# A two-block perceiver kernel on one Trainium2 core: the keys and values of every fourth sequence of the second cross-attention projected during the first feed-forward layer and kept in DRAM

## What is computed

```
x = x + L0_xattn(layernorm(x), ctx)
x = x + L0_attn(layernorm(x))
x = x + L0_ffn(layernorm(x))
x = x + L1_xattn(layernorm(x), ctx)
x = x + L1_attn(layernorm(x))
x = x + L1_ffn(layernorm(x))
```

```
def act_qdq(x):
    scale = max(max(abs(x)) / 32767, 1e-12)
    return clip(round(x / scale), -32768, 32767) * scale
...
x = act_qdq(x);  up = act_qdq(x @ w_up.T);  gate = act_qdq(x @ w_gate.T)
sig = round(sigmoid(gate) * 65536) / 65536
gate = act_qdq(gate * sig);  o = act_qdq(gate * up)
return o @ w_down.T
...
q = x1 @ Wq.T + bq;  k = x2 @ Wk.T + bk;  v = x2 @ Wv.T + bv
attn = softmax(q k^T / 4) per head;  return (attn v) @ Wo.T + bo
```

## Time and profile before

| what | value |
|---|---|
| median of 3 runs | 1647.59 us (1645.24 to 1649.38) |
| the profiled execution | 1646.64 us |
| its span on the core | 1644.9 us |
| PE, PEld busy | 1472.1 us (89%), 1131.8 us (69%) |
| DVE, ACT, POOL busy | 898.0 us (55%), 718.2 us (44%), 498.4 us (30%) |
| mean granted clock of TensorE | 0.967 |
| the chain that ended last, by engine | PE 71%, DVE 16%, issue 5%, POOL 4%, ACT 3% |

### The profile page before, as it was taken

How to read it: one execution, slowest core, us unless ns; L and a number is a source line. 1 busy time by engine, 2 the same in 40 slices (tenths; PEclk the granted TensorE clock), 3 DMA queues, 4 the chain that set the end, 5 groups by cost and what they waited for, 6 DMA issues and landing times.

```text
span 1644.9 us, 32798 instructions
## 1 busy us (share of the span) xinstructions
PE 1472.1 (89%) x12556; PEld 1131.8 (69%) x12556; DVE 898.0 (55%) x1896; ACT 718.2 (44%) x1761; POOL 498.4 (30%) x693
## 2 busy tenths in 40 slices
PE   3999996982899999999995788789999999999999
PEld 3877774432777777777773566538876885886787
DVE  3898896388445555655554778734224323422432
ACT  3887775486445555555551555422212211221221
POOL 2345551001036855854551878500000000000000
PEclk9999999995999999999996999989999999999999
DMA  7000000001031151135100000013421340342230
GB/s 280 21 10 2 1 0 1 1 0 34 7 129 46 60 221 38 45 141 204 39 25 1 1 1 0 1 45 112 157 103 45 136 178 13 134 150 87 90 135 13
DMA packets 49501, 111.39 MB, mean 68 GB/s; under 512 B 4240, under 2 KB 6800, under 8 KB 46864
## 3 DMA queue, kind: packets, MB, share of 16 engines
q1 hardware_dynamic: 49424, 110.36, 19.1%
HBM read 99.86 MB, written 10.49 MB: 67 GB/s over the span
## 4 chain that ended last, share of the span: by engine, by line
PE 71%; DVE 16%; issue 5%; POOL 4%; ACT 3%; DMA 1%; SPq 0%; DVEq 0%; POOLq 0%; ACTq 0%
PE ps L831 22%; PE ps L479 14%; PE ps L677 7%; PE ps L683 7%; PE ps L485 4%; PE ps L703 4%; PE ps L882 3%; DVE R L1491 3%; PE ps L714 2%; PE ps L655 2%; DVE amax L1373 2%; DVE nmx L1251 1%; DVE R L1442 1%; DVE R L1410 1%; PE ps L579 1%
## 5 line engine op out<-in xcount | busy, mean ns | idle before, releaser
L831 PE MATMUL ps<-R 128*128 128x256 f32 x1792 | 388.6, 379 | 3.5 <-DVE R L1620 3.5
L831 PEld LDWEIGHTS ps<-R 128*128 128x128 f32 x1792 | 340.0, 190 | 52.3 <-issue 6.5
L479 PE MATMUL ps<-R 128*128 128x128 f32 (+1 forms) x1344 | 307.4, 388 | 6.4 <-DVE R L1369 4.8
L479 PEld LDWEIGHTS ps<-R 128*128 128x128 f32 x1344 | 190.4, 194 | 119.6 <-issue 109.4
L1752 POOL TENSOR_TENSOR R<-R,c_inv 128x1024 f32<-128x1024 f32 x64 | 121.1, 1893 | 186.4 <-DVE c_inv L1528 186.4
L1090 ACT ACTIVATE R<-ps,c_nmx 128x257 f32<-128x257 f32 x256 | 118.0, 474 | 99.1 <-DVE c_nmx L1515 99.1
L1491 DVE COPY R<-ps 128x512 f32<-128x512 f32 x128 | 88.3, 690 | 106.8 <-PE ps L703 105.6
L677 PE MATMUL ps<-R,x_wk 128*128 128x256 f32 x512 | 128.8, 394 | 0.0
L683 PE MATMUL ps<-x_wv,R 128*128 128x256 f32 x512 | 121.1, 379 | 0.0
L1828 POOL TENSOR_SCALAR g_ve<-g_mv 128x4 f32<-128x4 f32 x4 | 0.9, 236 | 345.9 <-DVE g_mv L1582 345.9
L677 PEld LDWEIGHTS ps<-R,x_wk 128*128 128x128 f32 x512 | 92.7, 191 | 16.9 <-issue 0.8
(11 more groups left out here) (198 smaller groups left out, 2486.8 us busy)
## 6 DMA issues: line engine op xcount, KB each, us to landing
R<-quadrant_sums SPq DMA_DIRECT2D x32, 1024.0 KB, 6.9
R<-in_f_hq SPq DMA_DIRECT2D x32, 768.0 KB, 4.6
R<-in_ctxT SPq DMA_DIRECT2D x64, 257.0 KB, 2.7
R<-in_f_hq SPq DMA_DIRECT2D x8, 1024.0 KB, 8.2
quadrant_sums<-R SPq DMA_DIRECT2D x8, 1024.0 KB, 8.2
R<-in_f_w SPq DMA_DIRECT2D x3, 1024.0 KB, 7.0
R<-in_ctxk SPq DMA_DIRECT2D x16, 128.0 KB, 2.1
out<-x SPq DMA_DIRECT2D x4, 512.0 KB, 2.6
```

Source lines behind the costliest of these rows:

```text
L479: r = mm(dst, w[:, ki, fo * P:(fo + 1) * P], src[:, ki, :], start=(ki == 0), stop=(ki == KI - 1))
L831: r = mm(ps[:, 4 * (g % 2) + bk, half * HALF:(half + 1) * HALF], f_wr[g % 3][:, w, ki * P:(ki + 1) * P], src[:, k, ki, :], start=(ki == 0) ...
```

## The change

Sequences 3, 7, 11, ... (u = 3 of each tile, 16 in all) are no longer projected in the loop. They are numbered j = 0 to 15 and projected in `L0_ffn`: j = 0 to 9 between the gate and up projections and `c_last`, 10, 11 and 12 after `f0_down(0)`, `(1)` and `(2)`, and 13 to 15 after `f0_down(3)`. For each, SP loads the context (`load_ahead`), GpSimd shifts it (`shift_ahead`), TensorE projects it, ACT copies keys and values into one of three small buffers (`stage_ahead`), and SP stores both in the DRAM tensor `kv_ahead` (`store_ahead`). In the loop SP loads keys and values of tile i back, 256 KB each, into `c_kT[3]` and `c_v[3]`. Step u = 1, which projected u = 3, now projects nothing. At u = 2 the first half of the values stands ahead of the turning. Some semaphores are merged, and `ctx_last` is loaded at the start of the program.

```diff
@@ SP
+            def load_ahead(j):
+                sp.dma_start(a_ctx[j % 3], A["ctxT"][SPT * j + 3, :, :, 0:S - 1]).then_inc(ctxk_in[j % 3], 16)
+            def store_ahead(j):
+                sp.wait_ge(k_copied, ahead_no(j))
+                sp.dma_start(kv_ahead[j, :, 0:2, :], a_kT[j % 3]).then_inc(ahead_stored[j % 3], 16)
+                sp.wait_ge(v_copied, ahead_no(j))
...
+            for j in range(AHEAD):
+                if j + 3 < AHEAD:
+                    sp.wait_ge(v_ready, ahead_no(j))
+                    load_ahead(j + 3)
+                if j == 3:
+                    sp.wait_ge(f0_gj, 2)
...
+                if j >= 1:
+                    store_ahead(j - 1)
@@ PE, c_step
-                more = not (last and u >= 2)
+                more = u != 1 and not (last and u >= 2)
...
+                if more:
+                    pe.wait_ge(v_copied, rest_no(done - 1))
+                    if u == 2:
+                        c_values((u + 2) % SPT, 0)
                 if behind:
                     pe.wait_ge(c_nrm, n)
                     c_turn_probs(n - 1, (u + 1) % 2, 0)
                 if more:
-                    pe.wait_ge(v_copied, n + 2)
-                    for c in range(2):
+                    for c in range(1 if u == 2 else 0, 2):
                         c_values((u + 2) % SPT, c)
@@ PE, around f0_down
+            for j in range(AHEAD_PAUSE):
...
+                    pe.wait_ge(v_copied, ahead_no(j - 4))
+                keys_ahead(j, 2 * (j % 4))
+                values_ahead(j, 2 * (j % 4) + 1)
...
             f0_down(0)
+            ahead(10)
             f0_down(1)
+            ahead(11)
             c_turn(0)
             f0_down(2)
+            ahead(12)
             c_query(0)
             f0_down(3)
+            for j in range(13, AHEAD):
+                ahead(j)
@@ ACT
-            for f in range(3):
+            for f in range(2):
                 f0_up_int(f)
             act.wait_ge(f0_scale, 4)
...
+            for f in range(2, NF0):
+                stage_ahead(f, 2 * (f % 4))
+                f0_up_int(f)
+                f0_gate_int2(f)
+            for j in range(NF0, AHEAD_PAUSE):
+                stage_ahead(j, 2 * (j % 4))
@@ POOL
-            for k in (QX, QG, QU, QS):
-                all_max(k)
+            all_max(QX)
+            pool.wait_ge(c_last_in, 16)
+            for j in range(3):
+                shift_ahead(j)
+            all_max(QG)
+            shift_ahead(3)
+            all_max(QU)
+            shift_ahead(4)
+            all_max(QS)
+            for j in range(5, AHEAD_PAUSE):
+                shift_ahead(j)
...
             for u in range(3):
                 c_shift(u, 0)
+            for j in range(AHEAD_PAUSE, 13):
+                shift_ahead(j)
             all_max(QO)
```

More of the change, by code:

```diff
@@ L202, in perceiver, with ahead_no, first_no, rest_no @@
         c_nmr = sb("c_nmr", [P, 1])
+        AHEAD, AHEAD_PAUSE = T, 10
+        def ahead_no(j):
+            return j + 1 if j < AHEAD_PAUSE else j + 3
+        def first_no(u):
+            return AHEAD_PAUSE + u + 1
+        def rest_no(m):
+            return AHEAD + m + 1
+        def ahead_shift_no(j):
+            return j + 1 if j < AHEAD_PAUSE else j + 4
+        a_ctx = [view(WT + 4608 + 512 * i, KI, S - 1) for i in range(3)]
+        a_kT = [view(WT + at, KI, S - 1) for at in (0, 1024, 1536)]
+        a_v = [view(WT + at, 512) for at in (512, 2560, 2048)]
         HALF, QUAD = BLK // 2, 4 * BLK
@@ L358, in perceiver @@
         N1 = 2 * T
+        NORMS = 4 * T
         WOUT = {X0: x0_wo, A0: a0_wout, A1: a1_wout}
@@ L433, in _ @@
                     n = SPT * i + u
-                    sp.wait_ge(v_ready, n + 1)
-                    sp.dma_start(c_ctx[u], A["ctxT"][n + SPT]).then_inc(ctx_in[u], 16)
+                    if u < 3:
+                        sp.wait_ge(v_ready, rest_no(3 * i + u) if i or u == 2 else first_no(u))
+                        sp.dma_start(c_ctx[u], A["ctxT"][n + SPT]).then_inc(ctx_in[u], 16)
+                    if u == 1 and i:
+                        load_keys(i)
+                    if u == 3 and i:
+                        load_values(i)
                     if n == 3:
@@ L902, in _ @@
         def _(act):
-            for m in free["act"]:
+            for m in ():
                 act.sem_inc(m, 1)
@@ L1095, in c_step @@
                 c_exps(u % 2, n)
-                more = not (last and u >= 2)
+                more = u != 1 and not (last and u >= 2)
                 if more:
-                    c_keys(u % 2, n + 2)
-                if more:
+                    m = rest_no(3 * i + 2 if u == 0 else 3 * i + u + 1)
+                    c_keys((u + 2) % SPT, m)
                     after(act, c_o, n - 1)
-                    c_values((u + 2) % 4, n + 2)
+                    c_values((u + 2) % SPT, m)
                 if u == 1 and not last:
@@ L1534, in _ @@
             f0_add(0)
-            for u in range(2):
+            for u in (0, 1, 3):
                 r = v.tensor_copy(c_kT[u][:, :, S - 1], colb[:, BK1, :])
@@ L1748, in c_step @@
                 n = SPT * i + u
-                if not (last and u >= 1):
-                    c_shift((u + 3) % SPT, i + (u + 3) // SPT)
+                if u >= 1 and not last:
+                    c_shift(u - 1, i + 1)
                 pool.wait_ge(c_rinv, n + 1)
@@ L1771, in _ @@
                 c_shift(u, 0)
+            for j in range(AHEAD_PAUSE, 13):
+                shift_ahead(j)
             all_max(QO)
             c_rsqrt(0)
+            shift_ahead(13)
             c_bias(0)
+            for j in range(14, AHEAD):
+                shift_ahead(j)
             for u in range(SPT):
```

196 lines of the change are left out of this document (134 added, 62 removed).

## The result

| | before | after |
|---|---|---|
| median | 1646.69 us (1645.24 to 1649.38, 4 runs) | 1699.24 us (1698.77 to 1700.09, 4 runs) |
| span of the profiled execution | 1644.9 us | 1697.4 us |
| mean granted clock of TensorE | 0.967 | 0.955 |
| first scores of the loop (n = 0) | 464.27 | 505.00 |
| from there to the scores of n = 62 | 403.1 | 415.4 |

The changed kernel takes 1.0318 times as long (95% interval 1.03 to 1.0336), 52.5 us more. The forecast was 1683 us and the range 1660 to 1694: the direction was right, the time is 16 us above the forecast and 5 above the range.

The account below looks back on a forecast made before the run. Bound by waits for DVE, ACT and GpSimd's maxima before the down projection, by TensorE in it, by DVE's chain in the loop. 1646.64 + 21.2 + 21.9 - 7.2 = 1682.5, median 0.95 higher: 1683 us; range 1660 to 1694.

Parts of the forecast that it names:

- GpSimd's switches: In L0_ffn, changing between maxima and ordinary operations costs 7.04 us each way; QO and f0_down(0) come 21.2 us later.
- The last link: Ahead of QO: load 12, needing the projection of j = 9, lands near 425.5, shift 12 ends near 426.5, QO starts 433.5.
- (a): In L0_ffn, the switch towards the maxima is free, only the one away from them costs: 1663 us, chance 0.17.
- (b): In L0_ffn, the switches hide altogether, since GpSimd loads while it waits: 1660 us, chance 0.07.
- The six late projections: In the down projection, j = 10 to 15 are paid in full on TensorE: 6 x 3.65 = 21.9 us.
- that switch: GpSimd's switch behind QO stays, but one more projection ahead of c_turn(0) hides it; no size was given.
- The step without clock: In the loop, the thinned step u = 1 takes 6.44 us instead of 7.06, saving 0.62, clock changes aside.
- the loop's term of - 7.2 us: In the loop, u = 1 saves 0.62 and u = 2 loses 0.17: 0.45 a tile, 7.2 us over 16 tiles.
- rival (c): The clock falls in the thinned loop step: 1.8 us more in half of the tiles, some 15 us, 1698 us; chance 0.11.
- the prediction's own signs of being wrong: QS starting before 385, steps u = 1 under 5.5 us, or a clock granted below full in the loop.
- the row that I priced the clock by: Loop step n = 62, taken as such a thinned step: the scores behind it take 0.84 us instead of 0.69.
- a collision: In L0_ffn, DVE multiplying while GpSimd shifts, both from SBUF: up to 1.04 us each, at most five times, range only.

Follow-up runs that it names:

- e2_noshift: The changed kernel without the subtraction of the last context row for the first ten early sequences: 1691.67 us, ratio 1.025.
- e9_together: The changed kernel with the next tile's first keys in u = 1, their shift in u = 0, early shifts 3 to 9 on DVE, 10 to 12 behind QO: 1656.08 us.
- e5_ten: The changed kernel without the six projections between and behind the down projection's blocks, the loop loading the first tile's keys and values each time: 1679.85 us, ratio 1.0191.
- e7_spread: The changed kernel with keys projected in steps 0, 2, 3 and values one step later, in 0, 1, 2: 1704.96 us, ratio 1.0329.
- e11_fill4_behind: The changed kernel with four filler matmuls in step u = 1, behind the output projection and the first half of the turning: 1700.86 us, ratio 1.032.

## Why the prediction was wrong

- **GpSimd's switches: right.** Where nothing else was waited for, 7.0 to 7.3 us lay between a maximum and an ordinary operation, and 5.8 to 6.2 the other way. Taking 7.04 for both was 1.1 too much in one direction. QS and QO came within 0.4 us of the forecast and f0_down(0) is 21.2 late. That QO came out right was partly luck. The last link was forecast: load 12 behind the projection of j = 9, which ended at 421.4 (422.5 forecast). But TensorE's own projections led there, not ACT's queue, and the load took 4.8 us instead of some 3; shift 12 ended 0.8 us late (427.35), which the cheaper switch made up. (The row gives 3.17 / 3 = 1.06 for a shift, not 1.04; it changes nothing.) Rivals (a) and (b) fall for these switches; e2_noshift and e9_together show them as the cause. But (b) is right in one thing, which the forecast used without saying so: a switch can lie inside a wait. Ahead of the shift at 370.23 (load landed at 370.1) and, in the kernel before, ahead of the one at 390.76 (load issued at 387.94) it cost nothing, though an ISA row stands at both; ahead of `c_ve` it cost 7.04 all the same. Why these differ stays open.
- **The six late projections: right,** 20.7 (6 x 3.45) instead of 21.9, since the first half of a projection is 1.73 and not 1.92 between two blocks. e5_ten gives 21 back, 19.0 of it behind the start of the first block. The sum left out that TensorE's gap ahead of `c_turn(0)`, 1.5 us in the kernel before (440.19 to 441.70), is covered by the projections now, though the text had said that they would hide that switch.
- **The step without clock: right.** 6.44 was forecast, 6.44 to 6.45 measured wherever the clock is full; u = 2 is 6.39, 0.21 more than before where 0.17 was charged.
- **The clock: wrong.** The step that failed is the loop's term of - 7.2 us, with rival (c) at a chance of 0.11 and only "a part" of it in the range. The loop gave + 12.3 up to n = 62, and the clock below full in the loop was one of the prediction's own signs of being wrong. The missing 20 us are 1.3 to 2.5 us in twelve of the fourteen inner tiles. Rival (c) named the mechanism, and its 1698 is the measured time, but by other numbers: 1.8 us in half of the tiles. What costs is the output projection and the turning at half clock. The argument against it was that the output projection lies in the middle of the idle time. That is so by position, but it didn't help: of the two waits the longer one, 1.84 us, lies ahead of it and was filled with keys before (the other is 0.89, between the halves of the turning), so it is the first to run slowly. TensorE was busy 6.90 of 7.06 us in the full step and is busy 3.47 of 6.45 in the thinned one, and the trace of before had no such step but the last two. So the row that I priced the clock by was no measure for it, and the case called for a large chance and a bound of the range at 1698.

The Trainium skill, GPSIMD Engine Reference, section 2.1 (Instruction dispatch), gives a load of about 6 us (5.95 measured) for the first call of a freshly loaded kernel. The way towards the maxima agrees with it (5.88 and 5.83 in the chain) and the way back is over a us dearer (7.14). Here both were paid again at later changes, not only the first time.

What stays open: why tiles 7 and 12 keep the full clock, why every second tile does in e7_spread and e11_fill4_behind, and why a switch of GpSimd is hidden in one wait and not in another. The late maximum QU of e9_together (3.9 us behind the changed kernel's) has the cause told for e2_noshift: a granted clock of 0.50 from 257 to 270 us. So single executions differ by some us ahead of the stages that the change touches.

## What to carry to other kernels

Work that is taken out of an engine's wait may have been what kept TensorE's clock up: count, for a step that gets thinner, what runs first behind the now empty wait, price it at half clock, and give that case a large share. If work is to be spread, put it into the wait itself and check that its inputs are there by then; behind the wait it gained nothing here. And on GpSimd keep cross-partition maxima together: an ordinary operation between two of them cost up to 13 us (7.2 + 5.9) here, less where a wait covered a part.

## What was not expected of the hardware

- Four idle calls (1.99 us of matmuls that nobody reads) made the changed kernel 19 us faster, and a thinned step, whose TensorE work is 3.47 us at full clock, took longer (7.8 us) than the full one with 6.90 (7.06).
- The same fillers at two places of one step gave 1680.6 and 1700.9 us.
- While GpSimd shifted a context, DVE's integer product, 2.28 us by itself, took 2.97 us in the changed kernel; in e9_together a product beside two shifts took 3.12 and a subtraction 1.15 instead of 0.68. Other products kept their 2.28 us and the shift beside them took 2.4 to 3.1 us instead of 1.04, more than the 1.04 that the prediction allowed a collision.
